# The bucket stage of a two-layer graph kernel: runs fetched in pieces of 8 rows with three gathers and six buffers, in place of 16 rows, two gathers and four buffers

## The reference, cut to what matters

```
f1 = x[row]; f2 = x[col]
h1 = relu(f1 @ nbW + nbb); h2 = relu(f2 @ selfW + selfb)
log_alpha = concat([h1, h2]) @ attW + attb
gate = sigmoid(log(u) - log1p(-u) + log_alpha)      # u: noise of the edge
mask = clip(gate * (ZETA - GAMMA) + GAMMA, 0, 1)
d = clip((segment_sum(mask, row) + EPS_DEG) ** -0.5, 0, 10)
msg = (mask * d[row] * d[col])[:, None] * f2
x_next = segment_sum(msg, row)                      # over the 18750 nodes
```

## Time and profile before

| | before |
|---|---|
| median of 3 runs | 6465.84 us (6463.82 to 6478.51) |
| the profiled execution's own time | 6478.92 us |
| its span, first to last instruction | 6477.2 us |
| mean granted TensorE clock over the span | 0.68 of full speed |
| busy: PE, DVE, ACT, POOL | 69%, 83%, 39%, 18% |
| bucket stage, first gather to last matmul | about 743 us in layer 0, 740 us in layer 1 |

### The profile page before, as it was taken

One profiled execution on the slowest core, in us unless ns is written; L12 is line 12 of the kernel. 1 busy time (PEld: TensorE's weight loads), 2 busy tenths in 40 slices (PEclk: granted clock), 3 DMA queues, 4 the chain that ended last, 5 costly groups with the idle time before them and its releaser, 6 DMA issues. The chain is left out here.

```text
span 6477.2 us, 167839 instructions
## 1 busy us (share of the span) xinstructions
PE 4475.7 (69%) x58388; PEld 3985.0 (62%) x58388; DVE 5351.0 (83%) x10813; ACT 2500.7 (39%) x5126; POOL 1167.5 (18%) x1562
## 2 busy tenths in 40 slices
PE   3777777775878887355557777978885355557776
PEld 2666666664568886344446666578885344446666
DVE  8999999996469998999976666079998999976666
ACT  2556666662345554355510000445553355510000
POOL 0000000000013332000024443023332000034443
PEclk6777777775555555677778888555555677778888
DMA  2000000000356665799978888066665799979988
GB/s 67 0 0 0 0 0 0 0 0 13 8 201 233 233 233 172 268 330 330 330 235 242 238 238 224 0 206 231 231 231 164 279 330 330 330 237 246 247 248 225
DMA packets 438063, 1154.51 MB, mean 178 GB/s; under 512 B 211241, under 2 KB 216974, under 8 KB 437402
## 3 DMA queue, kind: packets, MB, share of 16 engines
q1 hardware_dynamic: 316671, 549.97, 26.9%
q0 software_dynamic: 75264, 350.72, 20.0%
q10 hardware_dynamic: 46036, 252.74, 10.3%
HBM read 932.05 MB, written 279.36 MB: 187 GB/s over the span
## 5 line engine op out<-in xcount | busy, mean ns | idle before, releaser
L1587 PE MATMUL psG<-y_window,area 128*128 128x64 bf16 x14976 | 666.1, 217 | 783.5 <-DVE area L1235 669.1
L1587 PEld LDWEIGHTS psG<-y_window,area 128*128 128x128 bf16 x14976 | 622.4, 114 | 827.4 <-issue 507.3
L1600 PE MATMUL psG<-work,edge 112*128 112x192 bf16 x7104 | 811.1, 278 | 360.4 <-DVE edge L1270 358.6
L1600 PEld LDWEIGHTS psG<-work,edge 112*128 112x128 bf16 x7104 | 732.1, 151 | 438.9 <-DVE edge L1270 367.7
L582 POOL DMA_INDIRECT work<-msg_d,widx x444 | 488.1, 1099 | 2125.2 <-issue 1580.3
L638 ACT ACTIVATE work<-iota,work 128x149 bf16<-128x149 f32 x2496 | 789.0, 406 | 0.0
L1409 PE MATMUL psG<-area,work 128*128 128x112 bf16 x2496 | 551.3, 390 | 339.7 <-DVE area L967 339.7
L1409 PEld LDWEIGHTS psG<-area,work 128*128 128x128 bf16 x2496 | 357.6, 149 | 488.2 <-issue 343.8
L1402 PE MATMUL psG<-work,merge 128*128 128x148 bf16 x4992 | 542.5, 293 | 70.0 <-ACT work L638 70.0
L1402 PEld LDWEIGHTS psG<-work,merge 128*128 128x128 bf16 x4992 | 525.8, 131 | 92.7 <-issue 66.8
L1270 DVE TENSOR_TENSOR edge<-y_edge,ids 112x2048 bf16<-112x2048 int16 x444 | 544.2, 1226 | 15.4
(11 more groups left out here) (254 smaller groups left out, 8172.2 us busy)
## 6 DMA issues: line engine op xcount, KB each, us to landing
msg_d<-work ACTq DMA_DIRECT2D x312, 776.0 KB, 4.5
area<-rlo_d SPq DMA_DIRECT2D x312, 512.0 KB, 4.2
merge<-crel_d SPq DMA_DIRECT2D x312, 512.0 KB, 5.0
area<-crelp_d SPq DMA_DIRECT2D x312, 512.0 KB, 5.7
y_window<-y_d SPq DMA_DIRECT2D x312, 48.0 KB, 3.5
work<-msg_d,widx POOLq DMA_INDIRECT x444, 15.4
y_d<-cur SPq DMA_DIRECT2D x7, 1008.0 KB, 3.8
y_d<-work SPq DMA_DIRECT2D x7, 1008.0 KB, 4.8
```

Of the source, the lines that this page charges most:

```text
L1587: ins = pe.matmul(psG[:, 2 * h + k // CH, k % CH * D:(k % CH + 1) * D], col_one_hots[:, h, k * P:(k + 1) * P], y_window[:, h, m * D:(m + 1 ...
L1600: ins = pe.matmul(psG[:, slot_, 0:MW], q_one_hots[slot_][0:WP, g, :, s], windows[slot_][0:WP, g, s, 0:MW], start=g == 0 and s == 0, stop=g ...
```

## The change

The constants change: WIN 16 to 8, WG 2 to 3 gathers, WP 112 places to 128 (all partitions), SLOTS 4 to 6. The places of a bucket are now: gather 0, the first 8 rows of tiles 0 to 127; gather 1, rows 8 to 15 of the same tiles, out of bounds for runs of at most 8; gather 2, in places 0 to 63 the third pieces (runs over 16), in places 64 to 71 the fourth pieces (over 24), in 72 to 99 the first and in 100 to 127 the second pieces of the last 28 tiles. The three gathers of a bucket share one semaphore; VectorE waits for all three, makes `ids` (24 a place) in one instruction and the one-hot matrix of 128 x 3072 in one instruction; TensorE does 24 matmuls for a bucket. In the setup, the ranking and moving is done for third and fourth pieces: the ranking matmuls get 294 columns in place of 147, and the moving gets two more matmuls for a bucket, with 8 weight columns.

```diff
-WIN = 16
-WG = 2
-WP = 112
-SLOTS = 4
-SPILL = WG * WP - T
+WIN = 8
+WG = 3
+SLOTS = 6
+THIRD, FOURTH = 64, P - 2 * TAIL
...
                 def load_windows(b):
+                    wait(pool, bucket_summed, n - SLOTS + 1)
                     for g in range(WG):
-                        wait(pool, half_summed, (n - SLOTS) * WG + g + 1)
                         pool.nop(nofuse=True)
                         pool.indirect_dma_start(
-                            out=windows[par][0:WP, g, :, :].rearrange("p s w -> p (s w)"), out_offset=None, in_=msg_d,
-                            in_offset=bass.IndirectOffsetOnAxis(ap=widx[0:WP, g, b:b + 1], axis=0),
-                            bounds_check=T * TR - WIN, oob_is_err=False).then_inc(windows_loaded[par][g], 16)
+                            out=windows[par][:, g * WIN:(g + 1) * WIN, :].rearrange("p s w -> p (s w)"), out_offset=None, in_=msg_d,
+                            in_offset=bass.IndirectOffsetOnAxis(ap=widx[:, g, b:b + 1], axis=0),
+                            bounds_check=T * TR - WIN, oob_is_err=False).then_inc(windows_loaded[par], 16)
...
-                dve.tensor_scalar(spills[h], runs[h], float(WIN), None, ALU.is_gt).then_inc(spills_ready, 1)
+                for k in range(2):
+                    ins = dve.tensor_scalar(spills[h][:, k * HI:(k + 1) * HI], runs[h], float((k + 2) * WIN), None, ALU.is_gt)
+                ins.then_inc(spills_ready, 1)
...
+            for h, (first, lanes) in enumerate(tiles):
+                dve.tensor_tensor(fourth_hots[h][0:lanes, :, :], iota[0:lanes, 0:FOURTH - THIRD].unsqueeze(1).to_broadcast([lanes, HI, FOURTH - THIRD]),
+                                  spill_slot[h][:, HI:2 * HI].unsqueeze(2).to_broadcast([lanes, HI, FOURTH - THIRD]), ALU.is_equal)
...
                 def bucket_hots(b, s, use):
                     n = L * HI + b
-                    for g in range(WG):
-                        dve.wait_ge(windows_loaded[s][g], use * 16)
-                        wait(dve, half_summed, (n - SLOTS) * WG + g + 1)
-                        dve.tensor_tensor(ids[0:WP, s, g * WIN:(g + 1) * WIN], windows[s][0:WP, g, :, MW].bitcast(i16),
-                                          shift[0:WP, g, bass.ds(b, 1)].to_broadcast([WP, WIN]), ALU.subtract).then_inc(ids_ready, 1)
-                        dve.wait_ge(ids_ready, n * WG + g + 1)
-                        dve.tensor_tensor(q_one_hots[s][0:WP, g, :, :], iota_rows[0:WP, :, :],
-                                          ids[0:WP, s, g * WIN:(g + 1) * WIN].unsqueeze(1).to_broadcast([WP, P, WIN]), ALU.is_equal).then_inc(q_hots_ready, 1)
+                    dve.wait_ge(windows_loaded[s], use * 16 * WG)
+                    wait(dve, bucket_summed, n - SLOTS + 1)
+                    dve.tensor_tensor(ids[:, s, :].rearrange("p (g s) -> p g s", g=WG), windows[s][:, :, MW].bitcast(i16).rearrange("p (g s) -> p g s", g=WG),
+                                      shift[:, :, bass.ds(b, 1)].to_broadcast([P, WG, WIN]), ALU.subtract).then_inc(ids_ready, 1)
+                    dve.wait_ge(ids_ready, n + 1)
+                    dve.tensor_tensor(q_one_hots[s], iota_rows.unsqueeze(1).to_broadcast([P, WG, P, WIN]),
+                                      ids[:, s, :].rearrange("p (g s) -> p g s", g=WG).unsqueeze(2).to_broadcast([P, WG, P, WIN]), ALU.is_equal).then_inc(q_hots_ready, 1)
...
-                    dve.memset(work[0:WP, :], 0.0).then_inc(windows_cleared, 1)
-                    dve.memset(area[0:WP, 0:WG * RW_], 0.0).then_inc(windows_cleared, 1)
+                    dve.memset(work[:, :], 0.0).then_inc(windows_cleared, 1)
+                    dve.memset(area[:, 0:2 * WG * RW_], 0.0).then_inc(windows_cleared, 1)
...
-                        ins = pe.matmul(psR[0:SPILL, 0, 3 * c:3 * c + 3], spill_hots[p_ % 2][h][0:lanes, b, :], row_parts[h][:, c, :], start=h == 0, stop=h == 1)
+                        pe.matmul(psR[0:THIRD, 0, 3 * c:3 * c + 3], spill_hots[p_ % 2][h][0:lanes, b, :], row_parts[h][:, c, :], start=h == 0, stop=h == 1)
+                    for h in range(2):
+                        lanes = (P, TAIL)[h]
+                        ins = pe.matmul(psR[THIRD:FOURTH, 0, 3 * c:3 * c + 3], fourth_hots[h][0:lanes, c, :], row_parts[h][:, c, :], start=h == 0, stop=h == 1)
...
-                        for g in range(WG):
-                            pe.wait_ge(q_hots_ready, n * WG + g + 1)
-                            for s in range(WIN):
-                                ins = pe.matmul(psG[:, slot_, 0:MW], q_one_hots[slot_][0:WP, g, :, s], windows[slot_][0:WP, g, s, 0:MW],
-                                                start=g == 0 and s == 0, stop=g == WG - 1 and s == WIN - 1)
-                            ins.then_inc(half_summed, 1)
+                        pe.wait_ge(q_hots_ready, n + 1)
+                        for r in range(WG * WIN):
+                            ins = pe.matmul(psG[:, slot_, 0:MW], q_one_hots[slot_][:, r // WIN, :, r % WIN], windows[slot_][:, r, 0:MW],
+                                            start=r == 0, stop=r == WG * WIN - 1)
+                        ins.then_inc(bucket_summed, 1)
```

More of the change, by code:

```diff
@@ L181, in build @@
         runs = [scratch[:, 296:296 + HI], scratch[0:TAIL, 443:443 + HI]]
[L182 to L187, removed]
+        spills = [scratch[:, 590:590 + HI].bitcast(bf16), scratch[0:TAIL, 738:738 + HI].bitcast(bf16)]
+        spill_slot = [scratch[:, 886:886 + HI].bitcast(bf16), scratch[0:TAIL, 1034:1034 + HI].bitcast(bf16)]
+        spill_row = [scratch[:, 1182:1182 + 2 * HI], scratch[0:TAIL, 1478:1478 + 2 * HI]]
+        row_parts = [area[0:lanes, at:at + 221].bitcast(bf16)[:, 0:3 * HI].rearrange("p (b m) -> p b m", m=3) for lanes, at in ((P, 0), (TAIL, 222))]
+        spilled, late_runs = scratch[:, 1774:1774 + HI], area[:, 444:444 + HI]
+        spill_hots = [[words(2 * NC + (2 * s + h) * PH * THIRD // 2, PH * THIRD // 2).bitcast(bf16).rearrange("p (b r) -> p b r", r=THIRD) for h in range(2)] for s in range(2)]
+        FW = HI * (FOURTH - THIRD) // 2
+        fourth_hots = [words(2 * NC + 2 * PH * THIRD + h * FW, FW).bitcast(bf16).rearrange("p (b r) -> p b r", b=HI) for h in range(2)]
         TB = (TBLOCKS + 1) * P
@@ L380, in _ @@
             sp.dma_start(tail_starts, start_d[P:T, :]).then_inc(starts_loaded, 16)
-            sp.dma_start(late_starts[SPILL:WP, :], start_d[WP:T, :]).then_inc(starts_loaded, 16)
+            for g in range(2):
+                sp.dma_start(late_starts[FOURTH + g * TAIL:FOURTH + (g + 1) * TAIL, :], start_d[P:T, :]).then_inc(starts_loaded, 16)
             whole = TBLOCKS * P * P
@@ L1009, in _ @@
-                link(dve.tensor_tensor(row_parts[h][:, :, 2], spill_row[h], row_parts[h][:, :, 1], ALU.subtract))
+                row = spill_row[h][:, 0:HI]
+                link(dve.tensor_tensor(row, first[:, 0:HI], window_row[0:lanes, h:h + 1].to_broadcast([lanes, HI]), ALU.add))
+                link(dve.tensor_copy(row_parts[h][:, :, 0], row))
+                link(dve.tensor_tensor(row, row, row_parts[h][:, :, 0], ALU.subtract))
+                link(dve.tensor_copy(row_parts[h][:, :, 1], row))
@@ L1035, in _ @@
+            link(dve.tensor_tensor(widx[:, 1, 0:HI], starts[:, 0:HI], runs[0], ALU.add))
             dve.sem_inc(span_ready, 1)
@@ L1434, in _ @@
             pe.wait_ge(spills_ready, 2)
-            pe.matmul(psR[:, 0, 0:HI], sides[:, 1, :], spills[0], start=True, stop=True)
+            pe.matmul(psR[:, 0, 0:2 * HI], sides[:, 1, :], spills[0], start=True, stop=True)
             for s in range(2):
-                pe.matmul(psR[0:TAIL, 1, 0:HI], sides[:, s, 0:TAIL], spills[0], start=s == 0, stop=False)
-            pe.matmul(psR[0:TAIL, 1, 0:HI], sides[0:TAIL, 1, 0:TAIL], spills[1], start=False, stop=True).then_inc(spills_ranked, 1)
+                pe.matmul(psR[0:TAIL, 1, 0:2 * HI], sides[:, s, 0:TAIL], spills[0], start=s == 0, stop=False)
+            pe.matmul(psR[0:TAIL, 1, 0:2 * HI], sides[0:TAIL, 1, 0:TAIL], spills[1], start=False, stop=True).then_inc(spills_ranked, 1)
             for p_ in range(PIECES):
```

78 lines of the change are left out of this document (45 added, 33 removed).

## The result

The changed kernel takes 6421.46 us (median of 5 runs, 6409.33 to 6431.88) against 6465.84 us (5 runs, 6457.16 to 6478.51): ratio 0.9929, interval 0.9909 to 0.9948. That is -44 us. I had forecast -85 us; sign and range hold, the size is half of it.

A forecast was written before the change was run, and what follows sets the result against it. Prediction: DMA transfers bound the bucket stages, with GpSimd becoming as tight after the change. Stages -132, memsets and first gathers +8, setup +39 sum to -85 us: 6381 us against 6465.8; range 6285 to 6540.

The forecast's parts named there:

- What bounds the kernel before: Both bucket stages before the change: transfers on the busiest DMA engine set the pace, 14 pieces x 0.362 = 5.07 us a bucket.
- The transfers: Bucket stages: 339 pieces, 1052 KB a bucket; 23.5 pieces of 0.186 us on the busiest DMA engine, 4.37 us.
- Rival A: Bucket stages: bytes alone count, the DMA engines set 4.35 us a bucket; 159 us faster, 6307 us; chance 0.19.
- Rival C: Bucket stages: a fixed 0.10 us for each gathered piece, 5.4 us a bucket; 150 us slower, 6616 us; chance 0.20.
- GpSimd: the step that failed: Bucket stages: GpSimd issues three gathers a bucket in 4.43 us, between 4.20 and 4.67, as tight as the DMA engines.
- two limits with jitter: Bucket stages: DMA at 4.37 and GpSimd at 4.43 us together give a period of 4.6 us, range 4.4 to 4.8.
- Rival B: Bucket stages: GpSimd's three gathers take 4.86 us a bucket and eat the gain; +1 us, about 6466; chance 0.13.
- VectorE and TensorE: Bucket stages: VectorE 2.5 us a bucket, its one-hot 1.76; TensorE's 24 matmuls 2.4 or 4.2 us; both covered by transfers.
- Six buffers: Bucket stages: six buffers cover a landing of 15.4 us in the median, against 6 x 4.6 = 27.6 us.
- The stages: Both bucket stages: 294 x (5.05 - 4.6) = -132 us, and +8 us for longer memsets and waiting for three first gathers.
- The setup: Before the stages: 294 added matmuls 32 us, VectorE 5.6 before them, 1.1 ahead of the sort; +39 us (37 to 49).
- Signs named beforehand: Profile signs of right (windows, DMA share, gathers, matmuls) or wrong (piece over 0.21 us, gathers well over 1.3, setup outside 37-49).

The follow-up runs named there:

- the small one-hot: Changed kernel with a bucket's one-hot cut from 128x3072 to 128x64 elements, sums left out, all gathers and matmuls kept: 6192.31 us.

## Why the prediction was right in sign and off in size

**What bounds the kernel before.** The forecast named the DMA queue, and the runs fit it. Shorter holds and 0.4 us more of VectorE a bucket (553.8 against 498.1 us in layer 0's stage) moved the kernel by 0.15%, so neither GpSimd nor VectorE sets its pace. TensorE, 72% busy, was not tested by a run in that kernel.

**The transfers.** Pieces and bytes a bucket were right (340, 1055 KB). The price was not: 0.166 us a piece, not 0.186, so 23.5 pieces take 3.9 us, not 4.37. (The 0.009 us that I took as fixed was a rate, 5101 packets in 3 us; by the same row's 186.8% a packet took 0.018 us. It changed little.) The gathers of before made 75264 / 588 = 128 packets each, those of the changed kernel 70560 / 882 = 80. The sizes of the single packets in the traces say why: before, 56482 packets have 6208 B, one piece each; after, 48606 have 6208 B and only 2696 have 3108 B. So nearly all of the small pieces travel in pairs, and no cost for each piece appeared. A packet of 6208 B took 0.364 us in the mean before and 0.328 after. Why it became shorter stays open; with the small one-hot it took 0.311 us though the DMA engines were busier, 86.5% in the window shown above, so it isn't that they had less to do. Rival A is out, since GpSimd and not the DMA engines set the period. Rival C, the slow side, is out: DMA busy fell to 0.75.

**GpSimd: the step that failed.** I put three gathers at 4.43 us, the middle of 4.20 (mean of before) and 4.67 (time by places). The places cost nothing, 1.00 against 0.98 us. But the mean of 1.10 in the earlier trace rows over a median of 0.98 in the earlier trace rows, which I took for outliers and carried over unchanged, was the holds: a longer one-hot makes longer ones. In the changed kernel they measured 0.27 us on each of three gathers, 0.8 us a bucket. 3 x (1.27 + 0.30) = 4.71 us, against the 4.6 I gave to two limits with jitter. In fact there was one limit, with the DMA engines well below it. The change did two things that made the holds dear: it made GpSimd the bound, and it joined two one-hots of 1.23 us into one of 1.76.

**Rival B** had the mechanism. "GpSimd eats it" at 4.86 us a bucket is what layer 1 nearly shows (710.8 / 147 = 4.84), and layer 0 shows 4.71. I gave it 0.13 since no row seemed to show holds. The timeline of before, read for gathers longer than 1 us against VectorE's rows beside them, could have:

```profile
3507.76 1.23 DVE L1270 TENSOR_TENSOR edge<-y_edge,ids 112x2048 bf16<-112x2048 int16 x1
3508.03 1.81 POOL L582 DMA_INDIRECT work<-msg_d,widx  x1 [2.71 <-PE psG L1600]
```

This gather ends at 3509.84, 0.85 us after the one-hot. The kernel came out faster and not level for two reasons: the two stages with their memsets gave 29 us more than B's -56 + 8 = -48 (layer 0 had 4.71 us a bucket and not 4.86), and the setup cost 32 us and not B's 49.

**VectorE and TensorE.** The one-hot is 1.76 us, as worked out. 24 matmuls take 2.24 us in the timeline where the granted clock is 1.0, and 3.58 where it is 0.59 in the mean, both below the period. Both are covered, as said, but "covered" counted only VectorE's time: its one-hot stood on the path all the same, by holding GpSimd.

**Six buffers** cover the landing, which fell to 4.5 us; four do as well.

**The stages** were forecast at -132 + 8 = -124 us, where the 8 hold a longer memset ahead of each stage. They gave -80.0 by first gather and last matmul, and the memsets 1.3 us each (3.94 in place of 2.65), so -77.4: 47 us off, mostly the period. **The setup** was forecast at +39 (37 to 49). The first gather comes 33.3 us later, 1.3 of it the memset, so the setup gave +32.0, below its range. The added matmuls cost 27.2 us, 0.092 each (a weight load of 8 columns takes 0.08 us, below my 0.10 a matmul), and VectorE ahead of them 4.0 in place of 6.7 us: the 1.1 us forecast ahead of the sort didn't show, since at 1529.9 us the changed kernel was 0.9 us earlier than the one before. The sum, -85, came to -47 in the profiled executions and -44 in the medians.

**Signs named beforehand.** Bucket windows 650 to 700 us: 693 in layer 0, right, but 711 in layer 1. DMA over 0.9: wrong, 0.75, and this alone says that the bound had moved. Gathers 3 to 4.4 us with little wait for TensorE: 3.75 and 3.87 us busy, right. 588 matmuls in 70 to 85 us: 69.6, just below. Of the signs of being wrong, two came: the setup's growth, 32 us, was outside 37 to 49, and the gathers were long, 1.27 us in the mean, while the DMA engines had time to spare, which is the sign for B short of its "well over 1.3 us".

## What to carry to other kernels

When an engine's mean is above its median, find out what its long instructions have beside them before you scale the mean; here 0.12 us on an engine with idle time became 0.27 us on the engine that sets the end. Taking most of it away was worth more than the whole change (157 against 44 us). Where GpSimd issues indirect gathers on the path, keep VectorE's instructions with two SBUF inputs short: cutting one of 1.76 us into six of 0.42 costs VectorE 0.3 us and gave 184 us here (6387.7 to 6203.7), while one input in PSUM removes the holds and costs speed. And when pieces are halved to save bytes, count the instructions that fetch them: the bytes fell 12%, the gathers rose by half, and the floor of three gathers (3.9 us) is now no lower than what the busiest DMA engine needs by an estimate (23.5 x 0.166 = 3.9 us, if the places spread evenly over the engines).

## What the runs showed of the hardware that I had not expected

- An indirect gather that is issued during a VectorE operation with two inputs in SBUF ends 0.85 to 0.88 us after that operation, for operations of 0.68, 1.23, 1.76 and 3.36 us alike; with one input in PSUM it takes its 1.00 us. (This is the one-hot of this kernel; no other two-input operation was tried.) A memset of 5.18 us, which reads nothing, doesn't hold them: the gathers beside it in the run with the small one-hot took 1.00 us, but for layer 0's first with 1.36 (1.34 or 1.36 in every run).
- A gather that starts together with the one-hot goes first: at 3519.72 us in the changed kernel one takes 1.00 us, and the one-hot that started at 3519.68 takes 1.82 us in place of 1.76.
- A gather's own time on GpSimd doesn't go by its places: 0.98 us for 112, 1.00 for 128, with 0.30 us to the next, with or without an empty instruction between.
- Two gathered pieces of 3104 B share a packet, and a piece takes 0.166 us of a DMA engine, less than half of the 0.362 us of one of 6208 B.
- Left open: why layer 1's stage is 18 us longer than layer 0's in the changed kernel (gathers of 1.29 against 1.25 us in the mean). In the kernels whose one-hots are split, small or read from PSUM the two differ by 0 to 8 us.
